# A mixture-of-experts loop on one Trainium2 core: 35 blocks of 256 rows, and 24 blocks of 256 with 11 of 128 between them

## The chip, the core and the metric

The kernel runs on one core of one Trainium2 chip (trn2). The metric is the device time of one execution in microseconds. The kernel before has a median of 1342.09 us in 3 runs (1334.37 to 1343.16).

## The reference

A decoder piece of four residual stages on x of 8 x 256 rows of 256 numbers. The change touches only the last stage, a mixture of 12 experts of which every row uses 3:

```python
gate_logits = jnp.einsum('bsd,de->bse', x, Wg)
topw, sel = jax.lax.top_k(gate_logits, 3)
topw = jax.nn.softmax(topw, axis=-1)
cw = jnp.einsum('bsk,bske->bse', topw, jax.nn.one_hot(sel, 12))
h = gelu(jnp.einsum('bsd,edh->ebsh', x, Wup) + bup[:, None, None, :])     # 256 -> 1024
y = jnp.einsum('ebsh,ehd->ebsd', h, Wdown) + bdown[:, None, None, :]      # 1024 -> 256
return jnp.einsum('bse,ebsd->bsd', cw, y)
```

The stages before it (cross attention, a second mixture in the attention's values and outputs, cross attention again) are computed by code that the change leaves as it is.

## The kernel before, in words

The stage has two parts. `route` normalizes the 2048 rows, computes the gates and the three best experts of each row, and gives each of the 6144 pairs of row and expert a place in a table. The places of one expert are consecutive and begin at a multiple of 256 (`BT`), so that a block of 256 places belongs to one expert. How many blocks an expert needs is known only on the chip, while the program has a fixed number of them: NB = (6144 + 12 x 255) // 256 = 35, which is enough for any routing. A block that is not filled, or not needed, is computed all the same, with a row of zeros in its empty places. VectorE finds the number of blocks of each expert, their running sums over the experts (L1906), each pair's place (L1909 to L1917), and the expert of each block, `expert_of` (L1919 to L1921). Once `expert_of` is there, SyncE loads the first weights. VectorE then writes one-hot tables of lane and column (L1927 to L1930), TensorE multiplies them into the list of rows of each block, `row_of` (L1843), and GpSimd gathers the rows of the first three blocks (L1619). The part ends with 16 idle products on TensorE (L1848).

`run_experts` is the loop over the blocks. Each operand is held as two f16 parts, high and low, and each product is three matmuls (`matmul3`, L82 to L84). In step j of the loop:

- **TensorE**: `up(j+1)`, 48 matmuls with 128x128 weights of the expert and 256 rows moving; `turn_rows(j+2)`, 8 transposes of the gathered rows (L2046); `down(j)`, 24 matmuls for each 128 rows, with the hidden values as the weights and 256 columns of the expert moving.
- **ScalarE**: the high part of the up weights of j+2 (L1654), 8 Gelus of block j+1 (L2015), the copy of the transposed rows of j+2 (L2008), the high part of the down weights of j+1 (L1660). Three steps are written out, 30 run in a hardware loop of two steps a turn (`run_blocks`), the rest is written out.
- **VectorE**: `output(j-1)`, which scales the result by the row's weight (L2109, once for each 128 rows); the low part of the up weights of j+2 (L1667); both parts of the hidden values of j+1 (L2097, L2099, four times each); the low part of the down weights of j+1 (L1672).
- **SyncE**: the up weights of j+3 and the down weights of j+2 (1 MB each), each as soon as VectorE has read the buffer that they go into. There are two buffers of each kind.
- **GpSimd**: the gather of block j+3, one DMA for each 128 rows (L1619), then the scatter of block j, which adds its rows to the result in HBM (L1993), one DMA for each 128 rows. Scatter j waits for `output(j)` and for the landing of scatter j-1, since both may add to one row. So gather j+3 is issued behind scatter j-1.

Each engine runs its own list in order; semaphore counts hold them together. Gathered rows have a ring of six buffers, outputs two, the Gelus' input four banks.

Of the kernel before, what the change touches and what calls it, by code (L numbers as in the profile page):

```python
# [25 lines left out]
P = 128  # L26
# [18 lines left out]
C = D // P  # L45
# [1510 lines left out]
LAST_TURN = (NB - 4) // 2  # L1556
# [5 lines left out]
COLUMNS = NB * TPB  # L1562
SHIFT = 8
# [14 lines left out]
def run_blocks(eng, slot):  # L1578

    for j in range(3):  # L1580
        slot(j, j % 2, j // 2)
    with eng.Fori(1, LAST_TURN) as i:
        slot(2 * i + 1, 1, i)
        slot(2 * i + 2, 0, i + 1)
    for j in range(2 * LAST_TURN + 1, NB):
        slot(j, j % 2, j // 2)
# [28 lines left out]
def gather_rows(pool, j, sem, xg, rows_in, row_of):  # L1615

    for ti in range(TPB):
        column = j * TPB + ti
        pool.indirect_dma_start(xg[j % RING][:, ti, :], None, rows_in[:, :],  # L1619
                                bass.IndirectOffsetOnAxis(row_of[:, column:column + 1], 0)).then_inc(sem(f"x_loaded{j % RING}"), 16)  # L1620


class ExpertWeights:
# [12 lines left out]
    def load_up(self, sp, j, par, turn=0, first=False):  # L1636
        e = sp.value_load(self.expert_of[0:1, bass.ds(j, 1)], min_val=0, max_val=E1 - 1)
# [5 lines left out]
    def load_down(self, sp, j, par, turn=0, first=False):  # L1643
        e = sp.value_load(self.expert_of[0:1, bass.ds(j, 1)], min_val=0, max_val=E1 - 1)
# [31 lines left out]
def route(nc, s, t, sem, ps, xt, xg, rows_in, row_of, expert_of, weights, ident16, out):  # L1676
# [14 lines left out]
    with ExitStack() as prep:  # L1691
# [15 lines left out]
        filled, blocks, sums = sb("filled", [P, E1], I32), sb("blocks", [P, E1]), two("sums", [P, SHIFT + E1])  # L1707
        ends, start = sums[1][:, SHIFT:SHIFT + E1], sb("start", [P, E1])
# [9 lines left out]
        past, expert_f = sb("past", [1, NB, E1]), sb("expert_f", [1, NB])  # L1718
# [138 lines left out]
        def _(dve):  # L1857
# [33 lines left out]
            dve.tensor_copy(nth_f[:], nth[:])  # L1891
# [49 lines left out]
def run_experts(nc, s, t, sem, ctx, ps, xg, xt, rows_in, row_of, ident16, out, weights):  # L1941
# [41 lines left out]
    def _(pool):  # L1983
        rows_of = out.rearrange("b s d -> (b s) d")
        pool.wait_ge(out_based, 16)
        for j in range(NB):
            if j + AHEAD < NB:
                gather_rows(pool, j + AHEAD, sem, xg, rows_in, row_of)
            pool.wait_ge(y_done, TPB * (j + 2))
            if j >= 1:  # L1990
                pool.wait_ge(y_added[1 - j % 2], 32 * ((j + 1) // 2))
            for ti in range(TPB):
# [3 lines left out]
        for par in range(2):  # L1996
            pool.wait_ge(y_added[par], 32 * ((NB + 1 - par) // 2))

    @block.scalar
    def _(act):  # L2000
# [5 lines left out]
        def rows_part(j, par, turn):  # L2006
            act.wait_ge(turned, 2 + j + 1)
            act.activation(xt[par][:].rearrange("p l c q -> p (l c q)"), T, ACT.Copy).then_inc(xt_split, 1)  # L2008
# [20 lines left out]
        run_blocks(act, slot)  # L2029

    @block.tensor
    def _(pe):
# [4 lines left out]
        def turn_rows(j, par, turn):  # L2037
            pe.wait_ge(x_loaded[j % RING], 16 * TPB * (j // RING + 1))
# [3 lines left out]
            for hl in range(2):  # L2042
                for c in range(C):
                    for ti in range(TPB):
# [4 lines left out]
        def up(j, par, turn):  # L2049
            pe.wait_ge(up_split, 2 + j + 1)  # L2050
            pe.wait_ge(xt_split, j + 1)
# [154 lines left out]
```

## Time and profile before

| | value |
|---|---|
| median of 3 runs (lowest, highest) | 1342.09 us (1334.37, 1343.16) |
| the profiled execution | 1335.52 us, its span 1333.8 us |
| granted TensorE clock over the span | 0.949 |
| PE, DVE, ACT, POOL busy | 85%, 83%, 66%, 28% of the span |
| issues of L1640 and L1647 (weights) | 35 each, 1024.0 KB each |
| gathers L1619, scatters L1993 | 70 each |

The page divides the span into 40 slices; the expert loop is the last ten of them or so. PE is the matmul engine, PEld its weight loads, DVE VectorE, ACT ScalarE, POOL GpSimd, and SP SyncE. Matmuls overlap, so the duration of one (about 0.27 us) is not its cost; the distance between two starts is.

### The profile page before, as it was taken

To read this page: it belongs to the slowest core of one execution; us is meant where nothing else is said; L and a number is where in the kernel's file an instruction comes from. 1 tells how busy PE (TensorE), PEld (TensorE's weight loads), DVE (VectorE), ACT (ScalarE), POOL (GpSimd) and SP (SyncE) were. 2 spreads that over 40 slices of the span, in tenths; PEclk is the share of its full clock that TensorE was granted. 3 is DMA by queue.
4 is the path that set the end of the run, shared out by engine and by line. 5 is a ranking of instruction groups with operands and counts; after the bars stand their busy time and mean duration, and the time that the engine had idled before them with its cause. 6 is when DMAs were issued, how large, how long until landed. Compare 5 with 4: busy or idle time off the path is not lost. (4 is left out here: it accounts for less than half of the span.)

```text
span 1333.8 us, 34600 instructions
## 1 busy us (share of the span) xinstructions
PE 1137.5 (85%) x13167; PEld 929.9 (70%) x13167; DVE 1101.4 (83%) x2341; ACT 885.7 (66%) x2039; POOL 367.5 (28%) x358
## 2 busy tenths in 40 slices
PE   2788866898999989999876777767999999999996
PEld 1666753676776767768645666644889989999895
DVE  6788876899999999998745888866888888888884
ACT  1898862586776767767715988732777777777772
POOL 7122201000000000000032222002366666666763
PEclk9999988899999999999988999756999999999999
DMA  7422201334335343353222222008677788888870
GB/s 224 111 74 59 61 23 44 96 80 110 115 79 156 74 108 115 82 152 75 69 75 74 74 59 60 25 0 274 217 237 231 233 241 237 241 239 243 232 204 3
DMA packets 209042, 170.31 MB, mean 128 GB/s; under 512 B 85661, under 2 KB 190274, under 8 KB 208882
## 3 DMA queue, kind: packets, MB, share of 16 engines
q1 hardware_dynamic: 193650, 146.88, 37.0%
q0 software_dynamic: 15232, 21.26, 7.5%
q8 instruction: 106, 1.74, 0.5%
q14 instruction: 54, 0.44, 0.1%
HBM read 126.13 MB, written 42.86 MB: 127 GB/s over the span
## 5 line engine op out<-in xcount | busy, mean ns | idle before, releaser
L1993 POOL DMA_INDIRECT out<-m_yo,m_xg x70 | 162.2, 2317 | 133.4 <-DVE m_yo L2109 118.3
L2015 ACT ACTIVATE m_hf<-m_ps,m_bue 128x256 f32<-128x256 f32 x280 | 117.3, 471 | 106.9 <-PE m_ps L84 106.9
L1181 ACT ACTIVATE f_pr<-f_ps,f_nb 128x256 f32<-128x256 f32 x256 | 108.0, 478 | 72.2 <-DVE f_nb L1464 71.7
L82 PE MATMUL m_ps<-m_ds,m_hs 128*128 128x256 f16 x560 | 152.6, 273 | 0.3 <-DVE m_yo L2109 0.3
L84 PE MATMUL m_ps<-m_ds,m_hs 128*128 128x256 f16 x560 | 152.6, 273 | 0.0
L83 PE MATMUL m_ps<-m_ds,m_hs 128*128 128x256 f16 x560 | 152.6, 273 | 0.0
L83 PE MATMUL m_ps<-m_xt,m_us 128*128 128x256 f16 x560 | 152.6, 273 | 0.0
L82 PE MATMUL m_ps<-m_xt,m_us 128*128 128x256 f16 x560 | 152.6, 273 | 0.0
L84 PE MATMUL m_ps<-m_xt,m_us 128*128 128x256 f16 x560 | 152.6, 273 | 0.0
L723 PE MATMUL x_ps<-ident,x_pr 128*120 128x128 f32 x512 | 82.3, 285 | 40.4 <-DVE x_pt L808 29.8
L1672 DVE SCALAR_TENSOR_TENSOR m_ds<-m_draw,m_ds 128x2048 f16<-128x2048 f32 x35 | 80.2, 2292 | 41.3 <-ACT m_ds L1660 41.3
L1133 POOL CAST f_mix_row<-f_mix 128x256 f16<-128x256 f32 x8 | 5.1, 638 | 372.7 <-DVE f_mix L1400 372.7
L1619 POOL DMA_INDIRECT m_xg<-expert_in,m_row_of x70 | 83.7, 1196 | 69.4 <-DVE m_row_of L1932 40.8
L2099 DVE SCALAR_TENSOR_TENSOR m_hs<-m_hf,m_hs 128x512 f16<-128x512 f32 x140 | 96.9, 692 | 4.8
L1468 DVE SCALAR_TENSOR_TENSOR f_pt<-f_ps,f_pt 128x512 f16<-128x512 f32 x128 | 87.5, 684 | 14.5 <-ACT f_pt L1151 14.5
L723 PEld LDWEIGHTS x_ps<-ident,x_pr 128*120 128x120 f32 x512 | 57.2, 141 | 58.7 <-issue 33.4
L82 PE MATMUL f_ps<-f_kt,f_qt 64*128 64x256 f16 x256 | 70.3, 276 | 30.0 <-ACT f_pr L1181 29.8
L808 DVE SCALAR_TENSOR_TENSOR x_pt<-x_ps,x_pt 120x512 f16<-120x512 f32 x128 | 87.7, 685 | 8.4 <-ACT x_pt L632 7.8
L1151 ACT ACTIVATE f_pt<-f_ps 128x512 f16<-128x512 f32 x128 | 79.1, 618 | 15.3 <-PE f_ps L84 15.2
L1464 DVE TENSOR_REDUCE f_nb<-f_ps 128x2 f32<-128x512 f32 x128 | 87.6, 685 | 2.0 <-PE f_ps L84 0.7
L623 ACT ACTIVATE x_pr<-x_neg,x_mx 128x120 f32<-128x120 f32 x256 | 80.1, 395 | 11.5 <-DVE x_mx L802 11.5
L1252 PE MATMUL f_ps<-ident,f_pr 128*128 128x128 f32 x512 | 83.6, 286 | 0.0
(386 smaller groups left out, 3872.2 us busy)
## 6 DMA issues: line engine op xcount, KB each, us to landing
m_uraw<-in_L_ffn_Wup SPq DMA_DIRECT2D x35, 1024.0 KB, 5.4
m_draw<-in_L_ffn_Wdown SPq DMA_DIRECT2D x35, 1024.0 KB, 5.8
head_values<-f_v_row SPq DMA_DIRECT2D x16, 520.0 KB, 5.1
f_vh<-head_values SPq DMA_DIRECT2D x16, 520.0 KB, 3.5
head_outputs<-f_at_row SPq DMA_DIRECT2D x16, 512.0 KB, 2.9
f_at_in_t<-head_outputs SPq DMA_DIRECT2D x16, 512.0 KB, 5.9
x_q_stack<-x_queries SPq DMA_DIRECT2D x48, 128.0 KB, 2.8
x_queries<-x_qt SPq DMA_DIRECT2D x16, 256.0 KB, 2.4
```

The lines of the kernel that those rows point to most:

```text
L82: pe.matmul(out, lhs[0], rhs[0], start=(n == 0), stop=False)
L83: pe.matmul(out, lhs[0], rhs[1], start=False, stop=False)
L84: last = pe.matmul(out, lhs[1], rhs[0], start=False, stop=(n == len(terms) - 1))
L723: last = pe.transpose(PT(u)[:, h, :], pr[u % 2][:, h, :], s.ident[:])
L808: dve.scalar_tensor_tensor(pt[u % 2][:, 1], PT(u), SPLIT, pt[u % 2][:, 0], ALU.mult, ALU.subtract).then_inc(pt_done, 1)
L1181: ins = act.activation(pr[h % 2][:, ti, :], S(h)[:, ti, :], ACT.Exp, bias=nb[h % 2][:, ti:ti + 1])
L1464: dve.tensor_reduce(nb[h % 2][:], S(h), AX_X, ALU.max, negate=True).then_inc(s_max, 1)
L1468: dve.scalar_tensor_tensor(pt[h % 2][:, 1].rearrange("p c t q -> p (c t q)"), PT(h), SPLIT, pt[h % 2][:, 0].rearrange("p c t q -> p (c t q)"),
L1619: pool.indirect_dma_start(xg[j % RING][:, ti, :], None, rows_in[:, :], bass.IndirectOffsetOnAxis(row_of[:, column:column + 1], 0)).then_in ...
L1993: pool.indirect_dma_start(rows_of, bass.IndirectOffsetOnAxis(xg[j % RING][:, ti, D:D + 1].bitcast(I32), 0), yo[j % 2][:, ti, :], None, bou ...
L2015: ins = act.activation(hf[:, q, m, :], U(q)[:, m, :], ACT.Gelu, bias=weights.bue[par][:, 2 * q + m:2 * q + m + 1], scale=UNSPLIT)
L2099: dve.scalar_tensor_tensor(hs[par][:, 1, 2 * q:2 * q + 2, :], hf[:, q], SPLIT, hs[par][:, 0, 2 * q:2 * q + 2, :], ALU.mult, ALU.subtract). ...
```

## The change

Places are now counted in half blocks of 128. An expert with 256k + r pairs gets k blocks of 256 and, for a rest of 1 to 128, one small place of 128; a rest of 129 to 255 gets another block of 256. The program has 24 blocks of 256 (`FULL`) and 11 of 128, 59 half blocks in all, which is enough for any routing. The small ones are j = 4, 7, 10, ... 34 (`HALVES`), every third from 4. In the table the 24 whole slots come first and the small ones behind them (`slot_of`, `column_of`). The experts' whole blocks fill the slots from the front, a whole one beyond the 24th takes two small slots, and the small rests follow, in whole slots as long as there are any (`level` and the minimum in the new VectorE lines). Each block still loads both weights of its expert.

```diff
-COLUMNS = NB * TPB
-SHIFT = 8
+FULL = TOP1 * TILES * P // BT
+HALVES = [j for j in range(NB) if j >= 4 and j % 3 == 1]
+COLUMNS = TPB * ((TPB * FULL + NB - FULL + 1) // TPB)
+SHIFT = 16
+EDGES = 2 * E1
...
+def tiles_of(j):
+
+    return 1 if j in HALVES else TPB
...
-    for ti in range(TPB):
-        column = j * TPB + ti
+    for ti in range(tiles_of(j)):
+        column = column_of(j) + ti
...
-            dve.tensor_copy(nth_f[:], nth[:])
+            chain(dve.tensor_scalar(second[:], nth[:], float(FULL), None, ALU.add))
+            dve.scalar_tensor_tensor(nth_f[:], nth[:], float(TPB), second[:], ALU.mult, ALU.min)
...
-            chain(dve.tensor_scalar(filled[:], TOTAL, float(BT - 1), None, ALU.add))
+            chain(dve.tensor_scalar(filled[:], TOTAL, float(P - 1), None, ALU.add))
             chain(dve.tensor_scalar(filled[:], filled[:], BT.bit_length() - 1, None, ALU.logical_shift_right))
-            chain(dve.tensor_copy(blocks[:], filled[:]))
+            chain(dve.tensor_copy(blocks[:, 0:E1], filled[:]))
+            chain(dve.scalar_tensor_tensor(blocks[:, E1:EDGES], blocks[:, 0:E1], float(BT), TOTAL, ALU.mult, ALU.is_lt))
             chain(dve.tensor_copy(sums[1][:, SHIFT:], blocks[:]))
-            for i, back in enumerate((1, 2, 4, 8)):
+            for i, back in enumerate((1, 2, 4, 8, 16)):
                 chain(dve.tensor_tensor(sums[i % 2][:, SHIFT:], sums[1 - i % 2][:, SHIFT:],
-                                        sums[1 - i % 2][:, SHIFT - back:SHIFT + E1 - back], ALU.add))
-            chain(dve.tensor_tensor(start[:], ends, blocks[:], ALU.subtract))
-            chain(dve.scalar_tensor_tensor(place[:], bcast_mid(start[:], TILES), float(BT), RANK, ALU.mult, ALU.add))
+                                        sums[1 - i % 2][:, SHIFT - back:SHIFT + EDGES - back], ALU.add))
+            dve.tensor_scalar(level[:], ends[:, E1 - 1:E1], float(FULL), None, ALU.max)
+            dve.tensor_copy(slots[:, 1, :], ends)
+            chain(dve.tensor_tensor(slots[:, 0, :], ends, blocks[:], ALU.subtract))
+            chain(dve.tensor_scalar(tiles_at[:], slots[:], float(TPB), None, ALU.mult))
+            chain(dve.scalar_tensor_tensor(tiles_at[:, :, E1:EDGES], slots[:, :, E1:EDGES], level[:], tiles_at[:, :, E1:EDGES],
+                                           ALU.add, ALU.min))
+            dve.tensor_tensor(jump[:], tiles_at[:, 0, E1:EDGES], tiles_at[:, 1, 0:E1], ALU.subtract)
+            chain(dve.scalar_tensor_tensor(over[:], bcast_mid(blocks[:, 0:E1], TILES), float(BT), RANK, ALU.mult, ALU.is_le))
+            chain(dve.tensor_tensor(over[:], over[:], bcast_mid(jump[:], TILES), ALU.mult))
+            chain(dve.tensor_tensor(over[:], over[:], bcast_mid(tiles_at[:, 0, 0:E1], TILES), ALU.add))
+            chain(dve.scalar_tensor_tensor(place[:], over[:], float(P), RANK, ALU.mult, ALU.add))
...
-            chain(dve.tensor_tensor(past[:], bcast(nth_f[:], E1), bcast_mid(ends[0:1, :], NB), ALU.is_ge))
+            chain(dve.tensor_tensor(past[:], bcast(nth_f[:], EDGES), bcast_mid(tiles_at[0:1, 1, :], NB), ALU.is_ge))
             chain(dve.tensor_reduce(expert_f[:], past[:], AX_X, ALU.add))
+            chain(dve.tensor_scalar(second[:], expert_f[:], float(E1), -float(E1), ALU.is_ge, ALU.mult))
+            chain(dve.tensor_tensor(expert_f[:], expert_f[:], second[:], ALU.add))
...
-            pool.wait_ge(y_done, TPB * (j + 2))
+            pool.wait_ge(y_done, TPB + tiles_until(j + 1))
             if j >= 1:
-                pool.wait_ge(y_added[1 - j % 2], 32 * ((j + 1) // 2))
-            for ti in range(TPB):
+                pool.wait_ge(y_added[1 - j % 2], 16 * tiles_through(j - 1, 2))
+            for ti in range(tiles_of(j)):
...
         def gelus(j, par, turn):
+            n = P * tiles_of(j)
...
-                    ins = act.activation(hf[:, q, m, :], U(q)[:, m, :], ACT.Gelu, bias=weights.bue[par][:, 2 * q + m:2 * q + m + 1],
+                    ins = act.activation(hf[:, q, m, 0:n], U(q)[:, m, 0:n], ACT.Gelu, bias=weights.bue[par][:, 2 * q + m:2 * q + m + 1],
...
-        run_blocks(act, slot)
+        for j in range(NB):
+            slot(j, j % 2, j // 2)
...
-                    last = matmul3(pe, U(q)[:, m % 2, :],
+                    last = matmul3(pe, U(q)[:, m % 2, 0:n],
...
-            for ti in range(TPB):
-                pe.wait_ge(y_done, TPB * j + ti + 1)
+            for ti in range(tiles_of(j)):
+                pe.wait_ge(y_done, TPB + tiles_until(j - 1) + min(ti + 1, tiles_of(j - 1)))
...
-                dve.tensor_scalar(hs[par][:, 0, 2 * q:2 * q + 2, :], hf[:, q], SPLIT, None, ALU.mult).then_inc(h_hi, 1)
+                rows = slice(0, n_rows)
+                dve.tensor_scalar(hs[par][:, 0, 2 * q:2 * q + 2, rows], hf[:, q, :, rows], SPLIT, None, ALU.mult).then_inc(h_hi, 1)
```

The low part of the hidden values, the copy of the transposed rows and the outputs are cut to the block's rows in the same way. What the lists of the engines look like now, at three places:

TensorE at the end of `up(4)` (`m_us0` is the weights' buffer, `m_xt0` the rows), the transposes of block 5 and the start of `down(3)`. Before:

```order
L84 MATMUL m_ps<-m_xt0,m_us0 128x256
L82 MATMUL m_ps<-m_xt0,m_us0 128x256
L83 MATMUL m_ps<-m_xt0,m_us0 128x256
L84 MATMUL m_ps<-m_xt0,m_us0 128x256
L2046 MATMUL m_ps<-m_ident16,m_xg5 128x128 x8
L82 MATMUL m_ps<-m_ds1,m_hs1 128x256
```

and of the change:

```order
L84 MATMUL m_ps<-m_xt0,m_us0 128x128
L82 MATMUL m_ps<-m_xt0,m_us0 128x128
L83 MATMUL m_ps<-m_xt0,m_us0 128x128
L84 MATMUL m_ps<-m_xt0,m_us0 128x128
L2086 MATMUL m_ps<-m_ident16,m_xg5 128x128 x8
L82 MATMUL m_ps<-m_ds1,m_hs1 128x256
```

The 48 matmuls of `up(4)` keep their number and their weights and move 128 columns in place of 256; `down(4)`, further on, has 24 matmuls in place of 48.

GpSimd around block 4 (ring buffer `m_xg4`), from the gather of block 6 to the scatter of block 5. Before:

```order
L1619 DMA m_xg0<-expert_in,m_row_of 128x272 x2
L1993 DMA out_0<-m_yo1,m_xg3 2048x256 x2
L1619 DMA m_xg1<-expert_in,m_row_of 128x272 x2
L1993 DMA out_0<-m_yo0,m_xg4 2048x256 x2
L1619 DMA m_xg2<-expert_in,m_row_of 128x272 x2
L1993 DMA out_0<-m_yo1,m_xg5 2048x256 x2
```

and of the change:

```order
L1637 DMA m_xg0<-expert_in,m_row_of 128x272 x2
L2027 DMA out_0<-m_yo1,m_xg3 2048x256 x2
L1637 DMA m_xg1<-expert_in,m_row_of 128x272
L2027 DMA out_0<-m_yo0,m_xg4 2048x256
L1637 DMA m_xg2<-expert_in,m_row_of 128x272 x2
L2027 DMA out_0<-m_yo1,m_xg5 2048x256 x2
```

The order is the same; block 4 has one scatter and block 7 one gather in place of two.

VectorE in the routing, from the blocks' counts to the places. Before:

```order
L1903 CAST m_blocks<-m_filled 128x12
L1904 COPY m_sums<-m_blocks 128x12
L1906 TENSOR_TENSOR m_sums<-m_sums 128x12 x4
L1908 TENSOR_TENSOR m_start<-m_sums,m_blocks 128x12
L1909 SCALAR_TENSOR_TENSOR m_place<-m_start,m_ps 128x192
```

and of the change:

```order
L1926 SCALAR_TENSOR_TENSOR m_blocks<-m_blocks,m_ps 128x12
L1927 COPY m_sums<-m_blocks 128x24
L1929 TENSOR_TENSOR m_sums<-m_sums 128x24 x5
L1931 TENSOR_SCALAR m_level<-m_sums 128x1
L1932 COPY m_slots<-m_sums 128x24
L1933 TENSOR_TENSOR m_slots<-m_sums,m_blocks 128x24
L1934 TENSOR_SCALAR m_tiles_at<-m_slots 128x48
L1935 SCALAR_TENSOR_TENSOR m_tiles_at<-m_slots,m_level,m_tiles_at 128x2x12
L1937 TENSOR_TENSOR m_jump<-m_tiles_at 128x12
L1938 SCALAR_TENSOR_TENSOR m_over<-m_blocks,m_ps 128x192
L1939 TENSOR_TENSOR m_over<-m_over,m_jump 128x192
L1940 TENSOR_TENSOR m_over<-m_over,m_tiles_at 128x192
```

There are more and wider links between the counts and the places. Behind them, the comparison for `expert_of` has 840 elements in place of 420 and two short instructions more, and `row_of` has 60 columns in place of 70.

## Rows read from the trace of the kernel before

**Rows 1.** Busy time by stretch (PE, PEld, DVE, ACT, POOL; clock, DMA share, GB/s).
```profile
960.00:970.00 10.00, 10.00 (x98) 9.01 (x96) 9.86 (x15) 7.05 (x10) 7.79 (x5) 1.00 0.90 269
1100.00:1200.00 100.00, 100.00 (x954) 90.05 (x952) 86.88 (x118) 72.02 (x103) 63.99 (x37) 1.00 0.82 238
```

**Rows 2.** Timeline of PE: start us, us, what; one step of the expert loop.
```profile
1212.75 0.61 PE L2046 MATMUL m_ps<-m_ident,m_xg 128*128 128x128 f16 x8
1213.19 0.27 PE L82 MATMUL m_ps<-m_ds,m_hs 128*128 128x256 f16 x1
...
1213.63 0.27 PE L83 MATMUL m_ps<-m_ds,m_hs 128*128 128x256 f16 x1
...
1215.92 0.27 PE L83 MATMUL m_ps<-m_ds,m_hs 128*128 128x256 f16 x1
```

**Rows 3.** Timeline of SP: two loads of down weights, 25 blocks apart.
```profile
1000.22 0.38 SPq L1647 DMA_DIRECT2D m_draw<-in_L_ffn_Wdown  x1
...
1274.14 0.38 SPq L1647 DMA_DIRECT2D m_draw<-in_L_ffn_Wdown  x1
```

**Rows 4.** Timeline of PE: first and last of 12 key-projection matmuls.
```profile
787.42 0.21 PE L82 MATMUL x_ps<-x_ct,w_k 128*128 128x120 f16 x1
...
788.00 0.22 PE L84 MATMUL x_ps<-x_ct,w_k 128*128 128x120 f16 x1
```

**Rows 5.** Timeline of DVE: one block of the expert loop.
```profile
1207.89 0.87 DVE L2109 TENSOR_SCALAR m_yo<-m_ps,m_xg 128x256 f32<-128x256 f32 x2
...
1210.95 0.42 DVE L2097 TENSOR_SCALAR m_hs<-m_hf 128x512 f16<-128x512 f32 x1
1211.41 0.69 DVE L2099 SCALAR_TENSOR_TENSOR m_hs<-m_hf,m_hs 128x512 f16<-128x512 f32 x1
...
1216.61 2.29 DVE L1672 SCALAR_TENSOR_TENSOR m_ds<-m_draw,m_ds 128x2048 f16<-128x2048 f32 x1 [1.32 <-ACT m_ds L1660]
1218.82 0.87 DVE L2109 TENSOR_SCALAR m_yo<-m_ps,m_xg 128x256 f32<-128x256 f32 x2
```

**Rows 6.** Timeline of ACT in the same block.
```profile
1213.03 0.84 ACT L2015 ACTIVATE m_hf<-m_ps,m_bue 128x256 f32<-128x256 f32 x2 [0.47 <-PE m_ps L84]
...
1214.66 1.92 ACT L1660 ACTIVATE m_ds<-m_draw 128x2048 f16<-128x2048 f32 x1
```

**Rows 7.** Timeline of POOL in the same block.
```profile
1209.59 2.93 POOL L1993 DMA_INDIRECT out<-m_yo,m_xg  x1 [3.04 <-DVE m_yo L2109]
...
1214.95 1.24 POOL L1619 DMA_INDIRECT m_xg<-expert_in,m_row_of  x1 [0.30 <-issue]
1216.49 0.98 POOL L1619 DMA_INDIRECT m_xg<-expert_in,m_row_of  x1 [0.30 <-issue]
```

**Rows 8.** What became of the row gathers of L1619.
```profile
DMA to landing us min/median/max: 2.8/3.7/7.3
```

**Rows 9.** Timeline of POOL: the two scatters that a DMA released.
```profile
962.14 1.80 POOL L1993 DMA_INDIRECT out<-m_yo,m_xg  x1 [0.30 <-issue]
...
968.94 2.74 POOL L1993 DMA_INDIRECT out<-m_yo,m_xg  x1 [1.29 <-DMA out<-m_yo,m_xg]
...
1070.46 1.80 POOL L1993 DMA_INDIRECT out<-m_yo,m_xg  x1 [0.30 <-issue]
...
1078.29 3.03 POOL L1993 DMA_INDIRECT out<-m_yo,m_xg  x1 [3.20 <-DMA out<-m_yo,m_xg]
```

**Rows 10.** Timeline of DVE in the routing.
```profile
904.14 0.78 DVE L1906 TENSOR_TENSOR m_sums<-m_sums 128x12 f32<-128x12 f32 x4
...
905.16 0.35 DVE L1909 SCALAR_TENSOR_TENSOR m_place<-m_start,m_ps 128x192 f32<-128x192 f32 x1
...
908.03 0.58 DVE L1919 TENSOR_TENSOR m_past<-m_nth_f,m_sums 1x420 f32<-1x420 f32 x1
```

**Rows 11.** Timeline of POOL: the last two scatters.
```profile
1324.04 1.55 POOL L1993 DMA_INDIRECT out<-m_yo,m_xg  x1 [2.28 <-DVE m_yo L2109]
1325.89 1.55 POOL L1993 DMA_INDIRECT out<-m_yo,m_xg  x1 [0.30 <-issue]
```

More of the change, by code:

```diff
@@ L1575, with tiles_until, tiles_through, slot_of @@
              *(f"x_loaded{i}" for i in range(RING)))
[L1578 to L1586, printed above, removed]
+def tiles_of(j):
+    return 1 if j in HALVES else TPB
+def tiles_until(j):
+    return TPB * j if j < 0 else sum(tiles_of(i) for i in range(j))
+def tiles_through(j, every):
+    return sum(tiles_of(i) for i in range(j, -1, -every))
+def slot_of(j):
+    halves = len([i for i in HALVES if i < j])
+    return FULL + halves if j in HALVES else j - halves
+def column_of(j):
+    return min(TPB * slot_of(j), slot_of(j) + FULL)
 def moe_stage(nc, a, s, out):
@@ L1706, in route @@
         top = sb("top", [P, 3, TILES])
-        filled, blocks, sums = sb("filled", [P, E1], I32), sb("blocks", [P, E1]), two("sums", [P, SHIFT + E1])
-        ends, start = sums[1][:, SHIFT:SHIFT + E1], sb("start", [P, E1])
+        filled, blocks, sums = sb("filled", [P, E1], I32), sb("blocks", [P, EDGES]), two("sums", [P, SHIFT + EDGES])
+        ends = sums[0][:, SHIFT:SHIFT + EDGES]
+        slots, tiles_at = sb("slots", [P, 2, EDGES]), sb("tiles_at", [P, 2, EDGES])
+        level, jump = sb("level", [P, 1]), sb("jump", [P, E1])
+        over = sb("over", [P, TILES, E1])
         slot_f, slot_i = sb("slot_f", [P, CHOICES]), sb("slot_i", [P, CHOICES], I32)
@@ L1717, in route @@
         nth, nth_f = sb("nth", [1, NB], I32), sb("nth_f", [1, NB])
-        past, expert_f = sb("past", [1, NB, E1]), sb("expert_f", [1, NB])
+        past, expert_f, second = sb("past", [1, NB, EDGES]), sb("expert_f", [1, NB]), sb("second", [1, NB])
         cwt = sb("cwt", [E1, TILES * P])
@@ L2051, in up @@
             pe.wait_ge(xt_split, j + 1)
+            n = P * tiles_of(j)
             for q in range(UP_PAIRS):
@@ L2062, in down @@
             pe.wait_ge(down_split, 2 + j + 1)
-            for ti in range(TPB):
-                pe.wait_ge(y_done, TPB * j + ti + 1)
+            for ti in range(tiles_of(j)):
+                pe.wait_ge(y_done, TPB + tiles_until(j - 1) + min(ti + 1, tiles_of(j - 1)))
                 matmul3(pe, Y(ti),
@@ L2095, in hidden @@
                 if q == 0:
-                    dve.wait_ge(y_ready, TPB * (j + 1))
-                dve.tensor_scalar(hs[par][:, 0, 2 * q:2 * q + 2, :], hf[:, q], SPLIT, None, ALU.mult).then_inc(h_hi, 1)
+                    dve.wait_ge(y_ready, 2 * TPB + tiles_until(j - 1))
+                rows = slice(0, n_rows)
+                dve.tensor_scalar(hs[par][:, 0, 2 * q:2 * q + 2, rows], hf[:, q, :, rows], SPLIT, None, ALU.mult).then_inc(h_hi, 1)
                 dve.wait_ge(h_hi, n + 1)
-                dve.scalar_tensor_tensor(hs[par][:, 1, 2 * q:2 * q + 2, :], hf[:, q], SPLIT, hs[par][:, 0, 2 * q:2 * q + 2, :],
-                                         ALU.mult, ALU.subtract).then_inc(h_done, 1)
+                dve.scalar_tensor_tensor(hs[par][:, 1, 2 * q:2 * q + 2, rows], hf[:, q, :, rows], SPLIT,
+                                         hs[par][:, 0, 2 * q:2 * q + 2, rows], ALU.mult, ALU.subtract).then_inc(h_done, 1)
         def output(j):
-            e = dve.value_load(weights.expert_of[0:1, j:j + 1], min_val=0, max_val=E1 - 1)
-            dve.wait_ge(x_loaded[j % RING], 16 * TPB * (j // RING + 1))
+            e = dve.value_load(weights.expert_of[0:1, slot_of(j):slot_of(j) + 1], min_val=0, max_val=E1 - 1)
+            dve.wait_ge(x_loaded[j % RING], 16 * tiles_through(j, RING))
             if j >= 2:
-                dve.wait_ge(y_added[j % 2], 32 * (j // 2))
-            for ti in range(TPB):
-                dve.wait_ge(y_ready, TPB * (j + 2) + ti + 1)
+                dve.wait_ge(y_added[j % 2], 16 * tiles_through(j - 2, 2))
+            for ti in range(tiles_of(j)):
+                dve.wait_ge(y_ready, 2 * TPB + tiles_until(j) + ti + 1)
                 dve.tensor_scalar(yo[j % 2][:, ti, :], Y(ti), xg[j % RING][:, ti, bass.ds(e + D + 1, 1)], UNSPLIT,
```

23 lines of the change are left out of this document (14 added, 9 removed).

## The prediction

> **What bounds the kernel now.** I first read the busy time by stretch. From 1100 to 1200 us the expert loop keeps PE busy for all of the 100 us at the full granted clock (1.00, the 2.4 GHz level), VectorE for 87, ScalarE for 72 and GpSimd for 64, with the DMA engines at a share of 0.82 and 238 GB/s; a shorter stretch near the start of the loop shows 269 GB/s at a share of 0.90 [rows 1]. So TensorE has the path, with VectorE and the DMAs not far below. Busy time of PE is not its cost, so I next took distances between starts from its timeline. From 1213.63 to 1215.92 lie 21 matmuls of 256 columns: 0.109 us each. The eight transposes of 128 columns take 0.44 us up to the next matmul, 0.055 each, although each has 128x128 weights of its own [rows 2]. A step of the loop is then 96 x 0.109 + 0.44 = 10.9 us. SyncE's list gives the period without any model: 25 blocks between 1000.22 and 1274.14, 10.96 us each, and two neighbouring outputs on VectorE are 10.93 apart [rows 3, 5]. TensorE's work fills its period, and nothing else does.
>
> Who has room? VectorE waits 1.32 us in each step, for ScalarE's high part of the down weights [rows 5]; its own work is 10.93 - 1.32 = 9.61 us. GpSimd waits 3.04 us for VectorE's output [rows 7]. Its gathers are issued at 1214.95 and 1216.49 and land 3.7 us later in the median [rows 8], so at 1220.2, while TensorE turns these rows one period after 1212.75, at 1223.7: a margin of 3.5 us.
>
> **The change, part by part. TensorE.** In a small block the 48 matmuls of `up` move 128 columns in place of 256. The nearest rows are the transposes (0.055 us) and twelve f16 matmuls of 120 columns, in the same pattern of three products, whose first and last start are 0.58 us apart: 0.053 each [rows 2, 4]. I take 0.055: 48 x 0.054 = 2.59 us less. `down` loses 24 matmuls, 24 x 0.109 = 2.62 us, and four transposes go, 0.22 us. That is 5.43 us a block and 11 x 5.43 = **59.7 us**. Of three blocks, 3 x 10.93 - 5.43 = 27.4 us are left to TensorE.
>
> The Trainium skill, page "TensorE: Matmul & The Clock Gate", section "Back-to-back issue gap", says that in a stream of weight load and matmul pairs the spacing at 128 columns is about 81 ns, as the load counts too. By it `up` would give back 48 x 26 ns = 1.25 us less per block, 13.7 us in all. The rows above speak against it, but their longest run here has only twelve matmuls.
>
> **VectorE.** The hidden values take 4.34 us (1210.95 to the end of work at 1216.61 - 1.32), in four pairs. In a small block an operation has half the elements. Two bounds: half the time, or none less. The output's operation with 256 elements takes 0.44 (0.87 for two), against 0.69 for the 512 of L2099 [rows 5]; I take 0.25 for that one and 0.12 for L2097, 1.5 us for the four pairs, and 0.4 for the second output. Three blocks then cost 3 x 9.61 - 1.9 = 26.9 us, below TensorE's 27.4. But not step by step: with `down` or `up` of a small block a TensorE step is 8.3 us and VectorE still has 9.6 to do in the step in which the small block's `down` runs. It falls behind by 1.3 us there and catches up in the third step. ScalarE: the high part of the down weights starts 1.63 us after the last Gelus (1213.03 to 1214.66) and does not shrink [rows 6]; it is off the path, since the low part it releases is not used until `down`, half a step later. What remains of the wait of 1.32 costs nothing as long as TensorE does not wait for VectorE. Unrolling ScalarE removes register arithmetic from an engine with 28 us idle in 100 [rows 1]: nothing, hidden by that idle time.
>
> **DMAs.** Weights are as before, 2 MB a block. Gathers and scatters add 0.28 + 0.26 MB to a whole block (128 rows of 272 numbers, 128 of 256, each twice) and half to a small one: 7.65 MB in three blocks, in place of 7.92. In 28 us that is 273 GB/s, against 238 now and 269 seen at a share of 0.90 [rows 1]. It fits, with little left. Both weight loads wait a whole step in their buffers before they are used, so they can land later; the row gathers can't.
>
> **GpSimd, where a new wait appears.** Scatter j may not start before scatter j-1 has landed, and gather j+3 is queued behind scatter j-1; TensorE's transposes wait for that gather, and with them all that follows. A whole block's two scatters take 5.06 us (1209.59 to 1214.95 - 0.30), one alone 2.93 [rows 7]. From the end of issue to the next scatter's start it was 5.00 us (962.14 + 1.80 to 968.94) and 6.03 us (1070.46 + 1.80 to 1078.29) in the two cases where the landing released it [rows 9]; in the others VectorE came later, so it was under 5.9 (10.93 - 5.06). Three blocks of this chain cost 2 x 5.06 + 2.93 + 3S = 13.05 + 3S, which equals TensorE's 27.4 at S = 4.8. At S = 5.0 it is 28.05. And the gather's margin of 3.5 us shrinks by 2.6 (half an `up` or half a `down` lies less between issue and use) and by up to 1.3 where VectorE is behind: about zero. Landings of up to 7.3 us [rows 8] are hidden today and will not be. I take the 0.65 us from S = 5.0 and 0.35 for late gathers, 1.0 us per three blocks, **11 us** in all. The bounds are 0 (S below 4.8) and 3.7 x 11 = 41 us (S always 6.03).
>
> **The routing.** Ahead of `expert_of` VectorE gets a link before the counts (0.2 us), the comparison, one more sum, two for `tiles_at` and two behind `past` (6 x 0.21, as the four sums take 0.2 each), three operations on 192 elements (3 x 0.39: 0.35 and the link), three short ones that no one waits for (0.3), and 420 elements more in two operations; from 192 elements in 0.35 to 420 on one partition in 0.58 [rows 10] that is 0.42 each. Sum 3.8 us. The narrower column table gives back 0.4. PE has only idle products there, so it is all on the path: **+3.4 us**. Bounds 2 and 5.
>
> **The end.** The last scatter started 2.28 us after the one before had been issued, by VectorE's output [rows 11]. The landing takes nearly that long or longer, so the 2.62 us that the last `down` loses turn into a wait: I give back 2.3. One scatter is issued in place of two, 1325.89 - 1324.04 = 1.85 us less.
>
> **Sum.** -59.7 + 2.3 - 1.85 + 3.4 + 11 = -44.9 us on the profiled execution's 1335.5: 1290.6. Of the three runs shown one is as short as that execution (1334.4), two are 7 us longer; the median of new runs should lie between 1290.6 and 1297. I say **1293**.
>
> **The rivals.**
> 1. *The chain of scatters and gathers sets the pace* (20%). With the DMA engines at 0.9 and more, landings come later than now: S near 6, which gives back 41 in place of 11, 1320 us; with S at 5.4, 1304. For it: the two rows of 5.0 and 6.0, and 273 GB/s. Against: these two are the only scatters of 70 that a landing released; at 238 GB/s VectorE came last otherwise.
> 2. *Weight loads hold up the short matmuls* (6%). Should `up` of a small block run at 0.081 us a matmul, 13.7 us less are saved, but part of the new wait goes into them: 1302. Against it, rows 2 and 4. That is the time by the skill's rule above.
> 3. *VectorE becomes the bound* (6%). If half-size operations cost as much as whole ones, three blocks take it 28.4 us, 1.0 over TensorE: 11 us more if added in full, 1304.
> 4. *Nothing gained* (3%). The loop is bound by the weights' stream, which does not shrink: then 10.9 us a block stay and only the routing is added, about 1337. Against it, 269 GB/s at 0.90.
> 5. *Slower* (2%). One mechanism: landings so late that the chain takes more than three periods of now. 13.05 + 3S reaches 32.8 at S = 6.6, and with the routing's 3.4 the kernel is 1% slower from S = 6.9 on, 1356 us. No row shows more than 6.03.
>
> **How the numbers follow.** The forecast has 63%, its own range 1279 (no new wait) to 1303. With rivals 2 and 3 and half of rival 1 the range 1278 to 1314 leaves out less than 2 in 10. A measurement of this kernel tells about 1% from no change, 13 us. Faster by that: the forecast and rivals 1 to 3, 94%. Within it 4%, slower 2%.
>
> **What would show it.** Starts of 128-column matmuls of `up` 0.054 us apart (0.081: rival 2). Three blocks, read from the weight loads, at 28 to 28.7 us (27.4: no new wait; 31: rival 1). Idle time before the transposes that a row gather ends, about 10 us in the loop; PE busy some 96%, the clock still 1.00. Idle time on TensorE ended by VectorE would speak for rival 3. DMA 265 to 275 GB/s. The first block's transposes 3.4 us later in the program. The prediction is wrong above all if S or the gathers' landings grow with the load.

## The result and the profile of the changed kernel

The changed kernel takes 1347.8 us in the median of its runs (1338.9 to 1353.8), the kernel before 1342.0 (1334.4 to 1350.5). The ratio is **1.0036, interval 1.002 to 1.0053**: no gain, and a loss of a third of a per cent, where 1293 us and a ratio of 0.963 were forecast. Even the range, 1278 to 1314, missed it.

The profiled execution of the changed kernel takes 1348.5 us, span 1346.8, against 1335.5 and 1333.8 before. Of these 13.0 us, 5.7 arise ahead of the expert stage, which the change doesn't touch; 2.7 come from the routing; and from the first block's transposes to the end of the span it is 404.5 us in place of 400.0. So a loop from which 60 us of TensorE's work were taken became 4.5 us longer.

Busy time by stretch, changed kernel (columns as in [rows 1]):

```profile
1000.00:1100.00 100.00, 89.70 (x871) 79.10 (x868) 83.79 (x121) 68.78 (x104) 61.16 (x31) 0.93 0.76 235
1100.00:1200.00 100.00, 88.88 (x840) 77.96 (x841) 78.69 (x111) 65.77 (x96) 57.77 (x30) 0.90 0.72 218
```

In [rows 1] PE was busy for all of the stretch, at a clock of 1.00. Now it is idle for 11 us in 100, its mean clock is 0.90, and every other engine and the DMAs do less than before in the same time. No unit is full: the loop is bound by a latency. The waits of the loop (1000 to 1300 us; total, times, longest) name it:

```profile
POOL out L2027 <- DVE m_yo L2152: 100.6, 18, 7.5
...
DVE m_ds L1690 <- ACT m_ds L1678: 50.6, 17, 5.8
...
ACT m_xt L2046 <- PE m_ps L2086: 34.3, 8, 5.5
PE m_ps L2086 <- DMA m_xg<-expert_in,m_row_of: 32.8, 8, 5.3
```

TensorE's transposes of L2086 wait eight times, 4.1 us each, for a gather of rows. The other three waits each stand behind that one: GpSimd waits for VectorE, VectorE for ScalarE, and ScalarE for TensorE's transposes. By the profile no scatter in this stretch waits for the landing of the scatter ahead of it. The timeline of PE around two of these waits:

```profile
1103.12 1.03 PE L2086 MATMUL m_ps<-m_ident,m_xg 128*128 128x128 f16 x8 [3.88 <-DMA m_xg<-expert_in,m_row_of]
...
1137.17 1.03 PE L2086 MATMUL m_ps<-m_ident,m_xg 128*128 128x128 f16 x8 [3.90 <-DMA m_xg<-expert_in,m_row_of]
1138.00 0.42 PE L82 MATMUL m_ps<-m_ds,m_hs 128*128 128x256 f16 x1
1138.21 0.42 PE L83 MATMUL m_ps<-m_ds,m_hs 128*128 128x256 f16 x1
```

These are the blocks 15 and 18, and the wait comes once in three blocks, for the blocks 9, 12, 15 and so on to 33. The two starts are 34.05 us apart. Three blocks were forecast at 28.4 and took 32.8 before. Behind each wait the matmuls of 256 columns are 0.21 us apart, in place of 0.109 in [rows 2]: TensorE works there at the lower of its two levels, 1.2 GHz, up to 1142.69, 5.5 us.

Why is the gather late? The chain of waits of the changed kernel, from the transposes of block 15 to those of block 18 (start, us, what; the matmuls are left out):

```profile
1103.12 1.03 PE m_ps L2086 x8
...
1114.97 0.60 ACT m_xt L2043
1115.57 1.81 ACT m_ds L1678
1117.40 0.32 DVE m_ds L1690
...
1119.61 0.16 DVE m_yo L2152
...
1121.30 3.49 POOL out L2027
1124.80 0.30 issue
1125.10 1.57 POOL out L2027
1126.67 0.30 issue
1126.97 2.34 POOL m_xg L1637
1129.31 0.30 issue
1129.62 7.51 DMA m_xg<-expert_in,m_row_of
1137.17 1.03 PE m_ps L2086 x8
```

This is a ring. The late transposes of block 15 hold up all that follows on TensorE, down to block 15's own matmuls, and these the last Gelus of ScalarE; behind them, in ScalarE's fixed order, stand the row copy and the high part of the down weights; behind that VectorE's low part and the output of block 14; behind that block 14's scatters; and in GpSimd's order behind these the gathers of block 18, for which TensorE waits next. Summed: 11.1 us on TensorE, 3.2 on ScalarE, 3.9 on VectorE up to the start of the scatter, 5.7 for two scatters, 2.6 for the first gather, 7.5 for the second up to its landing.

Two of these are longer than I had priced them. The timeline of POOL, then that of DVE, then the load issues of SP, all of the changed kernel:

```profile
1114.13 1.24 POOL L1637 DMA_INDIRECT m_xg<-expert_in,m_row_of  x1 [0.30 <-issue]
1115.67 1.05 POOL L1637 DMA_INDIRECT m_xg<-expert_in,m_row_of  x1 [0.30 <-issue]
...
1126.97 2.34 POOL L1637 DMA_INDIRECT m_xg<-expert_in,m_row_of  x1 [0.30 <-issue]
1129.62 2.72 POOL L1637 DMA_INDIRECT m_xg<-expert_in,m_row_of  x1 [0.30 <-issue]
```

```profile
1126.14 2.29 DVE L1690 SCALAR_TENSOR_TENSOR m_ds<-m_draw,m_ds 128x2048 f16<-128x2048 f32 x1
...
1129.19 2.29 DVE L1685 SCALAR_TENSOR_TENSOR m_us<-m_uraw,m_us 128x2048 f16<-128x2048 f32 x1
```

```profile
1128.60 0.38 SPq L1665 DMA_DIRECT2D m_draw<-in_L_ffn_Wdown  x1
1131.65 0.38 SPq L1658 DMA_DIRECT2D m_uraw<-in_L_ffn_Wup  x1
```

The gathers at 1114.13 and 1115.67 take 1.24 and 1.05 us. Those at 1126.97 and 1129.62 begin inside one of VectorE's long instructions and end at 1129.31 and 1132.34, which is 0.88 and 0.86 us after that instruction's end (1128.43, 1131.48), about a free gather's whole duration. So such an instruction of GpSimd doesn't get going until VectorE's has ended. And the end of either instruction of VectorE also frees a weight buffer: SyncE issues 1 MB each time, 0.2 us later. A held gather therefore ends, as a rule, 0.7 us behind the issue of a weight load (0.4 to 1.0; at the second gather of block 33 no load is left to issue). From block 6 on the gathers of the blocks 9, 12 ... 33 land 4.2 to 5.3 us after their own end, and those of the others 2.2 to 3.6.

Of the blocks 6 to 30 of the kernel before two, 13 and 29, have such a gather. In its timeline of POOL and of DVE, at block 13:

```profile
1061.91 1.24 POOL L1619 DMA_INDIRECT m_xg<-expert_in,m_row_of  x1 [0.31 <-issue]
1063.45 3.00 POOL L1619 DMA_INDIRECT m_xg<-expert_in,m_row_of  x1 [0.30 <-issue]
```

```profile
1063.31 2.29 DVE L1672 SCALAR_TENSOR_TENSOR m_ds<-m_draw,m_ds 128x2048 f16<-128x2048 f32 x1 [1.05 <-ACT m_ds L1660]
```

It ends 0.85 us after VectorE's instruction and landed 7.2 us after its start, where its neighbour took 3.1. TensorE waited 0.2 us for it. In the other blocks of before both gathers start ahead of L1672 and are free of it. Scatters are held in the same way, and in before already. The timeline of DVE ahead of the first scatter of [rows 7]:

```profile
1208.75 2.29 DVE L1667 SCALAR_TENSOR_TENSOR m_us<-m_uraw,m_us 128x2048 f16<-128x2048 f32 x1
```

That scatter begins at 1209.59, under this instruction, and ends at 1212.52, 1.48 us after it; the second one, free of it, took 1.82 us in place of 2.93. So the 2.93 us that the prediction took for one scatter had the hold in it.

### The profile page after: what moved, and what is told of

Read it like the earlier page. It is cut to its first block and busy times, and to the rows that moved or that the text cites. A ratio compares the mean times of both kernels' runs of the same rounds, so it can differ in the third digit from the quotient of the medians.

```text
span 1346.8 us, 33745 instructions
## 1 busy us (share of the span) xinstructions
PE 1106.7 (82%) x12859; PEld 896.2 (67%) x12859; DVE 1089.3 (81%) x2343; ACT 872.9 (65%) x2039; POOL 347.8 (26%) x336
## 5 line engine op out<-in xcount | busy, mean ns | idle before, releaser
L2027 POOL DMA_INDIRECT out<-m_yo,m_xg x59 | 131.2, 2225 | 159.4 <-DVE m_yo L2152 138.5
L2054 ACT ACTIVATE m_hf<-m_ps,m_bue 128x256 f32<-128x256 f32 (+1 forms) x280 | 107.9, 438 | 85.3 <-PE m_ps L84 83.9
L82 PE MATMUL m_ps<-m_ds,m_hs 128*128 128x256 f16 x472 | 138.2, 293 | 0.1
L83 PE MATMUL m_ps<-m_ds,m_hs 128*128 128x256 f16 x472 | 137.6, 292 | 0.0
L84 PE MATMUL m_ps<-m_ds,m_hs 128*128 128x256 f16 x472 | 137.3, 291 | 0.0
L82 PE MATMUL m_ps<-m_xt,m_us 128*128 128x256 f16 (+1 forms) x560 | 135.0, 256 | 0.0
L83 PE MATMUL m_ps<-m_xt,m_us 128*128 128x256 f16 (+1 forms) x560 | 135.0, 256 | 0.0
L84 PE MATMUL m_ps<-m_xt,m_us 128*128 128x256 f16 (+1 forms) x560 | 134.9, 256 | 0.0
L1690 DVE SCALAR_TENSOR_TENSOR m_ds<-m_draw,m_ds 128x2048 f16<-128x2048 f32 x35 | 80.1, 2290 | 59.4 <-ACT m_ds L1678 59.4
L1637 POOL DMA_INDIRECT m_xg<-expert_in,m_row_of x59 | 94.8, 1607 | 68.7 <-DVE m_row_of L1966 43.8
L2142 DVE SCALAR_TENSOR_TENSOR m_hs<-m_hf,m_hs 128x512 f16<-128x512 f32 (+1 forms) x140 | 85.8, 613 | 4.8
```

The lines of the kernel that those rows point to most:

```text
L82: pe.matmul(out, lhs[0], rhs[0], start=(n == 0), stop=False)
L83: pe.matmul(out, lhs[0], rhs[1], start=False, stop=False)
L84: last = pe.matmul(out, lhs[1], rhs[0], start=False, stop=(n == len(terms) - 1))
L2027: pool.indirect_dma_start(rows_of, bass.IndirectOffsetOnAxis(xg[j % RING][:, ti, D:D + 1].bitcast(I32), 0), yo[j % 2][:, ti, :], None, bou ...
L2054: ins = act.activation(hf[:, q, m, 0:n], U(q)[:, m, 0:n], ACT.Gelu, bias=weights.bue[par][:, 2 * q + m:2 * q + m + 1], scale=UNSPLIT)
```

## The experiments

The runs are told in the order of the argument, with ratios to the kernel before. "Per three" is the distance of the transposes of block 33 from those of block 6, divided by nine: 32.87 us before, 33.90 changed.

**Gathers one block further ahead.**

```
-AHEAD = 3
+AHEAD = 4
```

> The changed kernel with AHEAD = 4: each block's rows are gathered one step earlier, into a ring that already has six buffers. Theory A (the row gather of every third block comes too late, and the granted clock falls because TensorE waits for it): both go, three blocks take TensorE's own 27.4 us in place of 34.1, the clock stays at 1.00 in the loop and the kernel takes 1275 to 1290 us, 0.95 to 0.96 of the kernel before. Rival B (the DMA engines can't carry more than some 225 GB/s in this loop): the wait moves to the weights or to another gather, three blocks stay above 32 us, and the time stays above 1325 us.

Measured: 1287.8 us, **0.9622 (0.9561 to 0.9683)**, per three 27.38. The waits for gathers are gone. Busy time by stretch:

```profile
1100.00:1200.00 100.00, 100.00 (x1024) 90.88 (x1023) 96.92 (x138) 80.29 (x121) 68.51 (x37) 1.00 0.89 277
```

TensorE is full again at the full clock, at the 27.4 us of the prediction's sum. The gathers are no shorter (1727 ns in the mean, 1607 without this edit); they are only early enough. So all of the missing gain is in the wait for gathers and what it drags along.

This run also shows the ring that the prediction had priced. Of its waits (940 to 1240 us):

```profile
POOL out L2027 <- DMA out<-m_yo,m_xg: 37.1, 16, 4.2
```

Sixteen scatters wait here for the landing of the one ahead, up to 7.0 us from the end of its issue (1090.23 to 1097.26), which for that one is beyond the 6.6 us of rival 5, and TensorE stays full all the same. That ring is there, and it fits into 27.38 us.

**The same edit without the change.** `AHEAD = 4` in the kernel before:

> The kernel before with AHEAD = 4. Theory A: TensorE waits for row gathers for about 1 us in all of its loop, so nothing changes, 0.997 to 1.003. If gathering earlier were worth something by itself (shorter contention of GpSimd and VectorE), it would be 0.5% or more faster.

Measured: **1.0036 (1.0011 to 1.006)**, slightly above what was expected. The loop is the same, 10.93 us a block; the fourth gather stands in the routing ahead of the waits that start the loop, and there about 3 us are added: from VectorE's reading of the gates (899.40 us; before 892.93) to the first transposes it is 43.9 us in place of 40.9. So the gain of the run above is not a gain that before could have had: the wait is made by the change.

**VectorE's long instructions in four pieces each.** Four instructions of 128x512 in place of each 128x2048 of L1685 and L1690, such as

```
+        for k in range(4):
+            m = slice(2 * k, 2 * k + 2)
+            ins = dve.scalar_tensor_tensor(self.dsp[par][:, 1, m], self.draw[par][:, m], SPLIT, self.dsp[par][:, 0, m],
+                                           ALU.mult, ALU.subtract)
+        ins.then_inc(self.down_split, 1)
```

> The changed kernel with each of VectorE's two operations on 128x2048 numbers (low part of the up and of the down weights) written as four operations on 512. Theory C (GpSimd can't write a DMA's descriptors while a long VectorE operation runs, and this is what makes two gathers take 2.3 and 2.9 us in place of 1.2 and 1.0): every gather takes under 1.8 us, the wait of TensorE for the gather shrinks from 4 us to 1 to 2.5 us per three blocks, and the kernel takes 1305 to 1335 us. Rival D (gathers are slow because the DMA queues are loaded): their durations and the wait stay as they are, and the kernel takes 1345 us or more, as VectorE has 0.4 us more work in each block.

Measured: 1321.2 us, **0.9855 (0.9811 to 0.9899)**, per three 30.67. The gathers of this kernel in the loop (min, median and max of the duration in ns; us to landing), and then its load issues:

```profile
L1637 POOL DMA_INDIRECT m_xg<-expert_in,m_row_of x46: 981/1061/1501, 1006.0 to 1280.0; - x46
...
DMA to landing us min/median/max: 2.8/4.1/7.3
```

```profile
1119.51 0.38 SPq L1665 DMA_DIRECT2D m_draw<-in_L_ffn_Wdown  x1
```

No gather is held any more: the longest takes 1.50 us in place of 3.05. That is worth 3.2 us per three blocks. But the second gather of block 18 starts at 1119.93, 0.4 us behind that load, and still lands 7.3 us later, 6.3 after its end. At the blocks 9, 15, 24, 27 and 33, too, a load is issued before that gather's end; the load is then issued 0.7 to 1.4 us before that end, the gather lands 4.9 us after it or later, and TensorE waits 2.0 to 4.1 us. At 12, 21 and 30 the order falls otherwise: the load comes 1.7 us after the gather's start and 0.5 after its end, the landing 2.9 to 3.4 after its end, and TensorE doesn't wait. The hold is one cause, the weights' traffic another. Two things more are in these 3.2 us: the mean granted clock from 1100 to 1200 us is 0.95 in place of 0.90, and ten scatters of the loop now wait for a landing (23.6 us in all), which none did before this edit; they weren't separated. (The scatters remain long, 3.35 us at 1112.63 under the four pieces of L1687; why pieces free a gather but not a scatter wasn't followed up.)

**A quarter of the weights' bytes.** From the third load on each brings 256 KB in place of 1 MB; the rest of the buffer keeps older weights.

```
+        m = slice(0, 8) if first else slice(0, 2)
+        sp.dma_start(self.draw[par][:, m],
+                     self.a["L1_ffn_Wdown"][bass.ds(e, 1)].rearrange("o (m p) d -> (o p) m d", p=P)[:, m]).then_inc(self.d_loaded[par], 16)
```

> The changed kernel, in which each weight load of the loop from the third on brings only the first quarter of its columns (256 KB in place of 1024 KB); the rest of the buffer keeps older weights, so part of the computation uses wrong weights. All instructions of the engines keep their sizes. In the changed kernel the gathers of the blocks 9, 12, 15 ... land 4.2 to 5.3 us after the end of their instruction, and the others 2.2 to 3.6; the late ones have a weight load issued 1 us before they start and another 2 us after. Theory 'the rest of the lateness is the weights' traffic': landings after the end of the instruction fall to about 3 us, the instructions themselves keep their 2.3 to 2.9 us (held by VectorE), three blocks take 34.1 - 2 = about 32 us or a little less (31 if the clock drop goes too), ratio to before 0.975 to 0.99. Rival 'the landing is late since the gather's own descriptors are late or because of the scatter ahead of it, not by the weights': landings stay at 4 to 5 us, three blocks at 34 us, ratio 1.000 to 1.006.

Measured: 1310.1 us, **0.9781 (0.9719 to 0.9843)**, per three 30.14, below the 31 to 32 expected. The timeline of POOL has the same held gathers:

```profile
1112.20 2.34 POOL L1637 DMA_INDIRECT m_xg<-expert_in,m_row_of  x1 [0.30 <-issue]
1114.84 2.72 POOL L1637 DMA_INDIRECT m_xg<-expert_in,m_row_of  x1 [0.30 <-issue]
```

To the hundredth the durations of the changed kernel; but in the blocks 9, 12 ... 33 they now land 2.2 to 3.5 us after their end. The late part of the landing is thus the weights' traffic. What the smaller loads take from the scatters or from other waits is in the 3.8 us too, and so is the clock, 0.98 from 1100 to 1200 us in place of 0.90.

**Both together.**

> The same quarter loads, together with VectorE's two 128x2048 instructions in four of 128x512 each (part of the computation uses old weights). If the hold of GpSimd's DMA instructions by the long VectorE instructions and the weights' traffic are the two and only causes of the late gathers, both are gone: no wait of TensorE for a gather but for at most 1 us here and there, three blocks near 27.4 to 28.4 us as TensorE or VectorE asks (VectorE has 0.4 us more per block), ratio 0.960 to 0.972. If the order of the work alone makes the loop longer than TensorE's sum, three blocks stay at 30 us or more, ratio 0.98 and above.

Measured: 1294.6 us, **0.9638 (0.9579 to 0.9696)**, per three 28.31, which leaves 0.9 us over TensorE's 27.38; TensorE waits nine times for a gather, 0.8 us on average. VectorE is busy for 98.5 us in 100, and is probably the next bound there; no run shows it. The clock is back at 1.00. So the two causes together, with what follows from them, account for 5.6 of the 6.5 us by which three blocks are too long.

**TensorE kept busy in the wait.** 18 idle products into a free bank ahead of the transposes of the blocks that wait:

```
+            if j % 3 == 0 and j >= 6:
+                idle_products(pe, s, ps[:, 7, :], 18)
```

> The changed kernel with 18 idle products of 512 columns on TensorE ahead of the transposes of blocks 6, 9, 12 and so on, into a PSUM bank that is not used: 3.9 us of work in place of most of the wait for the gather. Theory A: the clock falls because TensorE stands idle there; with the filler it stays at 1.00, three blocks take 30.5 to 31.5 us in place of 34.1 and the kernel 1305 to 1320 us. Rival E (the clock falls for another reason, or the halved clock lies beside waits that would be there anyway): 1340 us or more.

Measured: 1338.0 us, **0.9967 (0.9943 to 0.9991)**, per three 32.43: a miss, 30.5 to 31.5 were expected. The timeline of PE at block 15:

```profile
1098.00 4.05 PE L91 MATMUL m_ps<-bo,e 128*128 128x512 f16 x18
1103.53 0.62 PE L2088 MATMUL m_ps<-m_ident,m_xg 128*128 128x128 f16 x8 [1.48 <-DMA m_xg<-expert_in,m_row_of]
```

The idle products end before the gather lands, so they delay nothing, and the granted clock is 1.00 all through the loop. Still only 1.5 of the 6.5 us come back. Its chain of waits shows where the rest stays:

```profile
1118.38 0.88 DVE m_yo L2154 x2
...
1127.83 8.49 DMA m_xg<-expert_in,m_row_of
```

From the transposes (1103.53) to block 14's output it is 14.85 us in place of 16.49, 1.6 less and not the 2.8 by which TensorE's own part got faster, because at the full clock the chain no longer goes through ScalarE but through TensorE's `down` of block 14. And of these 1.6 the gather's landing takes back 1.0 (8.49 in place of 7.51), while the first scatter is 0.5 shorter (2.94 in place of 3.49). I had counted the clock's price on its own: what it costs is only what it adds to the ring, and there something else was next.

**The small blocks last.** The change with its eleven small blocks at the end (24 to 34) in place of every third:

```
-HALVES = [j for j in range(NB) if j >= 4 and j % 3 == 1]
+HALVES = list(range(FULL, NB))
```

> The changed kernel (AHEAD = 3) with the eleven small blocks at the end, j = 24 to 34, in place of every third. Theory A: the 24 whole blocks run at 10.93 us without a wait, as before, so the harm comes from the order in which sizes alternate and not from small blocks as such; behind them each small block costs what VectorE needs, 7.7 to 8.6 us, more than TensorE's 5.5, so part of the gain is lost: 1310 to 1322 us, 0.977 to 0.986. Rival F (any small block makes its rows late, clock and all): small blocks cost 10 us or more, 1335 us or more.

Measured: 1312.2 us, **0.9773 (0.9746 to 0.98)**, within the range expected. The whole blocks keep 10.93 us each; the waits from 1190 us on, among the small ones:

```profile
POOL out L2027 <- DMA out<-m_yo,m_xg: 29.3, 7, 5.5
...
PE m_ps L2086 <- DMA m_xg<-expert_in,m_row_of: 15.3, 7, 3.4
```

The small blocks take 8.1 us each (1202.46 to 1283.29 for ten) where TensorE's work is 5.5, so half of the gain is lost there as well. But whole blocks lose nothing any more, where in the alternating order every three blocks pay for the ring. The number came out for a reason other than the expected one, which is luck: VectorE, busy for 74.8 us of the 81 from 1202 to 1283, isn't full. Six scatters in a row, from 1238.06 to 1276.55, are released by a landing, 7.7 us apart on average, 4.9 to 6.8 us after the one ahead was issued. Among small blocks the prediction's own ring, scatter behind scatter, thus seems to set the pace; no run separates it from the late gathers.

**ScalarE's loop unrolled alone**, in the kernel before:

> The kernel before with ScalarE's loop written out for all blocks and nothing else changed. ScalarE waits for TensorE in every step, so no theory gives it a price: 0.997 to 1.003. If the longer instruction stream cost fetches, it would be slower by more than that.

Measured: **1.0001 (0.9981 to 1.0021)**. This part of the change is worth nothing in time, as predicted.

**The version that keeps the gain.** `AHEAD = 4`, with the fourth gather taken out of the routing and put at the head of GpSimd's loop, ahead of its first wait:

```
-            for j in range(AHEAD):
+            for j in range(AHEAD - 1):
...
+        gather_rows(pool, AHEAD - 1, sem, xg, rows_in, row_of)
         pool.wait_ge(out_based, 16)
```

> AHEAD = 4 in the changed kernel, but the fourth gather is issued at the start of the loop's part, ahead of GpSimd's wait for the stored base of the result, so that the routing's part again ends behind three gathers. Theory A: the loop keeps its 27.4 us per three blocks and starts 3 us earlier than with four gathers in the routing's part: 1283 to 1287 us, 0.956 to 0.961. If the routing's part does not end on its gathers, it equals the run with AHEAD = 4, 0.962.

Measured: 1287.0 us, **0.9597 (0.957 to 0.9624)**, the fastest version tried, 55 us below the kernel before. Per three it is 27.38 again; the waits show none for a gather in the loop. Whether the place of the fourth gather adds anything over plain `AHEAD = 4` the intervals don't tell; in the traces it is 13.9 us from the first gather to the first transposes (931.57 to 945.47), against 17.5 with plain `AHEAD = 4` (922.09 to 939.60).

## Why the prediction was wrong

*TensorE's work: right.* Three blocks take 27.38 us where gathers are early, 27.4 predicted. The matmuls of `up` in a small block, timeline of PE of the changed kernel at the full clock:

```profile
1119.50 0.22 PE L82 MATMUL m_ps<-m_xt,m_us 128*128 128x128 f16 x1
...
1121.96 0.22 PE L84 MATMUL m_ps<-m_xt,m_us 128*128 128x128 f16 x1
```

45 rows lie from the one to the other, so 0.056 us each, where 0.055 was taken. Rival 2 is out. The rule of the Trainium skill ("TensorE: Matmul & The Clock Gate", section "Back-to-back issue gap", about 81 ns) doesn't hold for this stream, now over 45 matmuls and not only twelve.

*VectorE: right, but with too little meaning.* The four pairs of a small block take 2.9 us (1123.21 to 1126.14) in place of 4.34, so 1.4 are saved and 1.5 were predicted; in the run with `AHEAD = 4` VectorE is busy for 96.9 us in 100, which is 26.5 us in 27.38, where 26.9 were predicted. Rival 3 is out. But I asked of VectorE only whether it is full, not what its long instructions do to GpSimd.

*Unrolling and weight loads: right.* The loads land 5.8 and 6.1 us after issue, hidden.

*The routing: right.* 2.7 us up to the first transposes, 3.4 predicted (bounds 2 and 5). The five sums and the comparison, timeline of DVE:

```profile
910.07 1.06 DVE L1929 TENSOR_TENSOR m_sums<-m_sums 128x24 f32<-128x24 f32 x5
...
916.15 1.02 DVE L1951 TENSOR_TENSOR m_past<-m_nth_f,m_tiles_at 1x840 f32<-1x840 f32 x1
```

1.02 against 0.58 in [rows 10]: 0.44 for 420 elements more, 0.42 predicted.

*GpSimd: the step that failed.* "I take the 0.65 us from S = 5.0 and 0.35 for late gathers, 1.0 us per three blocks, 11 us in all." The measured term is 6.5 us per three blocks (33.90 - 27.38), 59 us over the nine measured, and so larger even than its upper bound of 41. Three things were wrong in it.

First, the ring was the wrong one. I closed it over scatter and scatter with the landing S between them, and rival 1 priced the same ring higher. In the loop of the changed kernel no scatter waited for a landing, and where sixteen did (`AHEAD = 4`) TensorE stayed full. The ring that sets the pace goes through the gather's landing, TensorE, ScalarE's order and VectorE's output. I saw its parts ("the gather's margin of 3.5 us shrinks ... about zero") and priced them at 0.35 us, as if a wait, once there, would end with its own length. But the wait delays the very work from which the next gather is released. A margin of zero in such an order must be priced as the length of the ring: 34.05 us with its real links. With the free gather durations of [rows 7] and the landing of 3.7 us of [rows 8] in place of the measured ones (1.1 and 3.8 us less), the way to the output at the full clock (1.6 less) and the two scatters of [rows 7] (5.06 us in place of 5.37, 0.3 less) it is 27.2 us, an estimate from these rows, just below TensorE's 27.4. So by this estimate the ring would have cost next to nothing, had its links kept the sizes of [rows 7] and [rows 8].

Second, these sizes are not constants. [rows 7] has gathers of 1.24 and 0.98 us that start ahead of VectorE's long instruction ([rows 5]: 1216.61). The change moves them by up to a few us against VectorE, under that instruction and into the weight load that its end sets off: 4.9 us more in the ring. [rows 8] held the warning, a landing of 7.3 us at most, and the prediction says that such landings "are hidden today and will not be", but 0.35 us per three blocks pays for few of them. They came to both gathers of every third block. The row of before at 1063.45 shows the cause, and I didn't ask why it was long. The Trainium skill has the rule, too: "SBUF — State Buffer", section "Who interferes with whom", says that a VectorE instruction with two SBUF inputs contends with a GpSimd instruction that reads SBUF, and the page's section "Summary: rules for kernel authors" adds that the one issued second is blocked until the first finishes. The gathers' rows agree (ends 0.85 to 0.88 us after VectorE's), and so does their part of the run with pieces; the scatters under four pieces, 3.35 us, aren't explained by it. The first of these sections also reports that `tensor_tensor`, which has two such inputs, did not stall a DMA, so the page gave a warning and no clear answer. I weighed neither.

Third, the clock. "The clock still 1.00" was forecast, and it fell to 0.90, since TensorE now idles for 4 us once in three blocks. By the run with idle products that is 1.5 us per three blocks (33.90 - 32.43) of the 6.5, and it isn't a term beside the other two but goes through the same ring.

*The end:* the last scatter waited 1.98 us for the landing ahead of it, as forecast.

*The chances.* "Slower" had 2% by one mechanism, landings beyond 6.6 us between scatters. That mechanism didn't occur, but the right one was outside of all five cases. The margin in the prediction's own working was zero, and with a zero margin on a ring a case "the gather sets the pace" with a price of several us per three blocks should have stood at a third or more.

## What to carry to other kernels

When a change shortens the engine that bounds a loop, follow every transfer that is issued inside the loop back to the work that releases it, and add up that ring, with the longest durations of each link and not the median: as soon as it is longer than the shortened period it sets the pace, and its waits feed themselves. A second look belongs to what overlaps what: durations of instructions of GpSimd and landings of transfers are those of one alignment, and an uneven step (here every third block) goes through all alignments. The remedy is cheap where buffers allow it, one more block of lead, and it should be part of such a change.

## What the runs showed of the hardware

An indirect DMA of GpSimd that begins under a 2.29-us instruction of VectorE ends 0.85 to 0.89 us (most gathers of the changed kernel's loop) or 1.5 us (scatter, 1121.30 to 1124.79 under L1685 at 1121.01) after that instruction's end. Under instructions of 0.62 us gathers take 1.50 us at most. In the changed kernel and the run with pieces a 128-row gather that ends 0.7 to 1.4 us after the issue of a 1 MB weight load lands 4.2 to 6.3 us after its end; with 256 KB loads it is 2.2 to 3.5. A load just ahead isn't the only case: with `AHEAD = 4` a free gather (1064.55, 0.99 us), whose end comes 4.0 us after a load, lands 4.8 us after its end, and why stays open. And behind waits of about 4 us, once in 34 us, TensorE's granted clock was at 1.2 GHz for about 5.5 us each time (blocks 9 to 30), in a loop where it had been 1.00 throughout.
